# A fused transformer block on one core: other places for the products beside gating and quantising, and a part of each group's end moved into the next steps

## The chip, the cores and the metric

The kernel runs on one core of a Trainium2 chip. The metric is the device time of one execution in microseconds. Engines are named as the profile names them: TensorE (PE, with PEld for its weight loads), VectorE (DVE), ScalarE (ACT), GpSimd (POOL) and SyncE (SP), whose queue issues all transfers.

## The reference, cut to what matters

The input x is 2 x 2048 rows of 512. Four residual stages follow each other; each begins with a layer norm.

```python
x = x + tanh(g0) * softmax((n(x) @ W.T + b) @ (ctx @ W.T + b).T) @ ctx              # stage 1, ctx 77 x 512
x = x + tanh(g1) * ternary(gelu(ternary(n(x), w_up)), w_down)                       # stage 2, 512 -> 2048 -> 512
x = x + tanh(g2) * (attention(n(x), ctx, 16 heads of 32, 77 keys) @ Wout + bout)    # stage 3
x = x + tanh(g3) * fp4(silu(fp4(n(x), gate_w)) * fp4(n(x), up_w), down_w)           # stage 4, 512 -> 2048 -> 512
```

`ternary` divides its input by the root of the row's mean square and multiplies by weights of -1, 0 and 1. `fp4` quantises its input and its weights in blocks of 16: a scale in an 8-bit format from the block's largest magnitude, then eight magnitudes for each number.

## The kernel before

The 4096 rows are 8 groups of 512 rows; a group is 4 tiles of 128 rows. Every engine runs its own list of instructions in order, written out by hand, and waits on semaphores (`want(engine, name, group, count)`). Each engine walks the same loop of two phases.

`phase_a(g3, g1)` has 26 steps. It does stage 3 of group g3 (`attend`, one step for four heads of a tile, 16 in all, each passing through scores, row maximum, Exp, transposes and values in later steps; then on3, ott, oth/otl, out3 and x3 for each tile) and stage 1 of group g1 = g3 + 1 (`stage1`; a tile starts at the steps of `START1`). After stage 1 it takes the statistics and norm of stage 2, transposes the four tiles (`T2_AT`), and computes the first up products (`UP_AT`). In its last steps it also quantises the first half of stage 4's input of g3 (`X4_STEPS`).

`phase_b(g, s4)` has 33 slots. It does stage 2 of group g (16 up products of eight matmuls with 512 columns each, 16 down products of the same size, norm 3 and the query products) and stage 4 of group s4 = g - 1. Stage 4 has 16 units. A unit is a gate product and an up product of four matmuls each (`gate_up`), a tanh on ScalarE (`tanh4`) and two multiplications on VectorE (`hidden`); the next gate product waits for the first of them, since it writes the same bank. After four units the tile's 2048 hidden numbers are quantised on VectorE (`quant4`, parts 0 to 4: block maxima, scales, scaling, codes, last multiplication), transposed by a DMA (`turn_h`), multiplied by w_down (`down4`, 16 matmuls) and added (`out4`). `TILE_AT` says at which slot a tile's units start, `QUANT_AT` and `POST_AT` where quantising and the product stand. In a slot TensorE first issues a whole up product, then a whole down product (four chunks of a tile), then the gate pair.

For stage 2, ScalarE makes two gelus and a square of every up product, and GpSimd subtracts the rounded gelu from the exact one (L430); SyncE transposes both parts (`turn_ht`, L311). GpSimd also makes the roots of the norms (`root`, L406; `root4`, L411; L417, L436). The order of SyncE's queue is `turns`: input codes' transposes (L332), those of the gelus, of the hidden codes (L339), a store of half a group (L349), and the load of the next group but one (`load_x`, L252), which waits for stage 2's results.

In group 0's phase B there is no stage 4. In its place VectorE makes the codes of the stage 4 weights in 36 parts (`prepare`), spread over the slots (`PREP_AT`), and SyncE transposes them (L302, L298).

The lines of the profile that matter: L1109 is the helper `product` (up, gate, w_down, query and others; told apart by the operand names), L1196 the down product, L877 and L881 the two multiplications of `hidden`, L512 tanh, L500 and L503 the gelus, L545 Exp, L835 to L859 quantising, L696 statistics, L709 variance, L727 norm, L733 the low half of transposed rows, L865 stage 4's norm, L901 `out4`, L930 row maximum.

## Time and profile before

| | |
|---|---|
| time, median of 3 runs | 1780.79 us (1778.44 to 1780.8) |
| the profiled execution's own time | 1780.83 us |
| its span | 1779.0 us |
| TensorE busy | 1356.1 us, 76% |
| VectorE busy | 1409.3 us, 79% |
| ScalarE busy | 692.7 us, 39% |
| GpSimd busy | 243.1 us, 14% |

The span runs from the first instruction to the last. TensorE's busy time overlaps from one matmul to the next, so its share overstates. Shares are means over all stages; a group takes about 191 us in the steady part (from 490 to 1636 us), the start takes 290 us and the end, without a next group, 143 us.

### The profile page before, as it was taken

The numbers are of one execution on the slowest core, as the hardware profiler recorded it, in microseconds if no ns is written. First come the engines' busy times: TensorE is split into PE (matmuls) and PEld (weight loads), VectorE is DVE, ScalarE is ACT, GpSimd is POOL, SyncE is SP. The second block draws the span as 40 slices with busy tenths as digits, with TensorE's granted clock in tenths as the row PEclk, the third lists the DMA queues.
The fourth block names the chain that finished last, engine by engine and source line by source line (L and its number), as shares of the span: only waits on it lengthen the run. The fifth ranks groups of instructions, "written<-read, shape, count | busy, mean of one in ns | idle before, by whom it ended". The sixth has DMA issues, their size and how long they took to land.

```text
span 1779.0 us, 22434 instructions
## 1 busy us (share of the span) xinstructions
PE 1356.1 (76%) x8120; PEld 695.2 (39%) x8120; DVE 1409.3 (79%) x2440; ACT 692.7 (39%) x2106; POOL 243.1 (14%) x197
## 2 busy tenths in 40 slices
PE   5043737889787988698878978798879887997775
PEld 4021314434363435343443435343534354343421
DVE  6988886877887787878887788779787888786786
ACT  2113205542374326442554236432734164414420
POOL 1102200031002200131003100320023001310000
PEclk9556867999899999999999989999999999999987
DMA  9165862043202410053104320342013300521002
GB/s 349 70 236 136 191 171 47 1 71 60 71 2 43 87 50 25 8 88 83 25 1 78 53 71 2 60 72 57 16 30 66 83 25 7 89 45 40 7 18 59
DMA packets 267428, 119.69 MB, mean 67 GB/s; under 512 B 244122, under 2 KB 244634, under 8 KB 265782
## 3 DMA queue, kind: packets, MB, share of 16 engines
q1 hardware_dynamic: 267318, 118.27, 28.5%
q8 instruction: 64, 1.05, 0.2%
q14 instruction: 46, 0.38, 0.1%
HBM read 49.04 MB, written 8.39 MB: 32 GB/s over the span
## 4 chain that ended last, share of the span: by engine, by line
DVE 45%; PE 33%; ACT 8%; issue 6%; DMA 4%; SPq 2%; POOL 0%; DVEq 0%; ACTq 0%
PE bank L1109 25%; PE bank L1196 6%; ACT region L545 4%; DVE amax L835 4%; DVE hid L840 3%; DVE pair L844 3%; DVE stats L696 2%; DMA hqt<-pair 2%; DVE region L935 2%; DVE th L877 2%; DVE pair L859 2%; DVE region L727 2%; DVE pair L852 2%; DVE sr L810 2%; SPq L302 1%
## 5 line engine op out<-in xcount | busy, mean ns | idle before, releaser
L1196 PE MATMUL bank<-w_dn,region 128*128 128x512 fp8e4 x1024 | 243.7, 386 | 41.6 <-DMA region<-region 41.6
L1109 PE MATMUL bank<-w_up,xt 128*128 128x512 fp8e4 x1024 | 247.6, 389 | 31.3 <-ACT region L503 16.6
L1109 PE MATMUL bank<-w_gate,xqt 128*128 128x512 bf16 x512 | 146.8, 414 | 99.4 <-DVE th L877 56.3
L430 POOL TENSOR_TENSOR region<-g,region 128x512 f16<-128x512 f32 x128 | 178.2, 1396 | 297.5 <-ACT region L503 289.8
L545 ACT ACTIVATE region<-bank,nm 128x77 f32<-128x77 f32 x512 | 161.0, 353 | 66.8 <-DVE nm L930 66.8
L512 ACT ACTIVATE th<-bank,each 128x512 f32<-128x512 f32 x112 | 77.0, 687 | 271.7 <-PE bank L1109 271.7
L877 DVE SCALAR_TENSOR_TENSOR th<-th,bank 128x512 f32<-128x512 f32 x112 | 76.8, 686 | 129.5 <-ACT th L512 129.5
L500 ACT ACTIVATE g<-bank 128x512 f32<-128x512 f32 x128 | 76.4, 597 | 246.9 <-PE bank L1109 188.4
L1196 PEld LDWEIGHTS bank<-w_dn,region 128*128 128x128 f16 x1024 | 101.5, 99 | 167.5 <-DMA region<-region 43.1
L1109 PE MATMUL bank<-w_down,hqt 128*128 128x512 bf16 x496 | 132.2, 427 | 43.8 <-DMA hqt<-pair 43.8
L1109 PEld LDWEIGHTS bank<-w_up,xt 128*128 128x128 f16 x1024 | 101.6, 100 | 162.2 <-ACT region L503 20.5
L1109 PE MATMUL bank<-w_gup,xqt 128*128 128x512 bf16 x512 | 145.6, 411 | 8.8 <-DVE xin L888 4.6
L1146 PE MATMUL bank<-ident,region 128*128 128x128 f32 x384 | 60.1, 296 | 102.5 <-DVE region L727 84.7
L477 ACT ACTIVATE xt<-bank 128x512 f16<-128x512 f32 x96 | 55.4, 600 | 179.8 <-PE bank L1146 179.7
L545 ACT ACTIVATION_READ_ACCUMULATOR region<-bank,nm 128x1 f32 x512 | 119.6, 235 | 0.0
L1109 PEld LDWEIGHTS bank<-w_gate,xqt 128*128 128x128 bf16 x512 | 49.2, 103 | 175.9 <-DVE th L877 71.6
L1109 PEld LDWEIGHTS bank<-w_down,hqt 128*128 128x128 bf16 x496 | 52.6, 108 | 119.9 <-issue 75.1
L930 DVE TENSOR_REDUCE nm<-bank 128x4 f32<-128x308 f32 x128 | 59.8, 472 | 49.4 <-PE bank L1109 49.3
L1109 PE MATMUL bank<-w_o,region 128*128 128x512 f16 x384 | 92.2, 392 | 8.6 <-DVE region L945 8.6
L536 ACT ACTIVATE region<-bank 77x512 f16<-77x512 f32 x128 | 79.0, 617 | 37.3 <-PE bank L1267 37.3
L1146 PEld LDWEIGHTS bank<-ident,region 128*128 128x128 f32 x384 | 48.0, 152 | 114.6 <-issue 75.3
L1109 PE MATMUL bank<-xt,w_q 128*128 128x512 f16 x384 | 88.1, 388 | 1.4 <-DVE xt L733 1.4
(208 smaller groups left out, 2468.5 us busy)
## 6 DMA issues: line engine op xcount, KB each, us to landing
xin<-in_x SPq DMA_DIRECT2D x16, 512.0 KB, 4.6
out_x<-x SPq DMA_DIRECT2D x16, 512.0 KB, 2.9
region<-in_w_up_t SPq DMA_DIRECT2D x1, 4096.0 KB, 13.7
hid<-in_gate_w SPq DMA_DIRECT2D x4, 1024.0 KB, 5.3
x<-in_gate_w SPq DMA_DIRECT2D x4, 1024.0 KB, 6.1
...
```

The lines of the kernel that those rows point to most:

```text
L430: eng.tensor_tensor(hn[1][:, t % 2, ns], g32[:, s % 2, :], hn[0][:, t % 2, ns], ALU.subtract).then_inc(sg["hl"], 1)
L477: eng.activation(xt[0][:, :, t * P:(t + 1) * P], bank[t % 2][:, :].rearrange("p (k t) -> p k t", k=KD), ACT.Copy).then_inc(sg[f"xh{stage}" ...
L500: eng.activation(g32[:, s % 2, :], bank[s % 2][:, :], ACT.Gelu).then_inc(sg["g32"], 1)
L512: eng.activation(th[:, u % 2, :], bank[4][:, :], ACT.Tanh, scale=half_cg[:, :]).then_inc(sg["th"], 1)
L536: eng.activation(pt3[0][0:M, m % 2], bank[6 + m % 2][0:M, :].rearrange("p (h t) -> p h t", h=HC), ACT.Copy).then_inc(sg["p3h"], 1)
L545: last = eng.activation(p3[:, n % 2, j, :], bank[4 + n % 2][:, j * M:(j + 1) * M], ACT.Exp, bias=nm3[:, n % 2, j:j + 1], accum_out=rs3[:, ...
L835: done(eng.tensor_reduce(peaks, blocks, AX.X, ALU.max, apply_absolute_value=True))
L877: eng.scalar_tensor_tensor(th[:, u % 2, :], th[:, u % 2, :], 1.0, bank[4][:, :], ALU.add, ALU.mult).then_inc(sg["hg"], 1)
L930: eng.tensor_reduce(nm3[:, n % 2, :], bank[4 + n % 2][:, 0:HC * M].rearrange("p (h m) -> p h m", h=HC), AX.X, ALU.max, negate=True).then_i ...
L1109: last = mm(out, lhs, rhs, start=(n == 0), stop=(n == len(pairs) - 1))
L1146: last = tr(bank[t % 2][:, k * P:(k + 1) * P], xn[:, t, k * P:(k + 1) * P], ident[:, :])
L1196: last = mm(bank[2 + t % 2][:, :], ht[i][:, t % 2, f, :], w_dn[:, f, :], start=(f == 0 and i == 0), stop=(f == KF - 1 and i == 1))
```

## The change

Sizes and number of products, transposes and transfers stay the same. Only their places in the lists of the engines change, with a few instructions split.

- Phase A: stage 1 starts one step earlier (`START1`). Statistics and norm of stage 1 are halved: tiles 0 and 1 stay in the phase B before, tiles 2 and 3 go to steps 2, 3 and 5. All four tiles of stage 2 are transposed in one step, tiles 2 and 3 through banks 4 and 5 (`state_bank`). Eight up products follow instead of three, in the steps 18 to 25, and ScalarE's gelus of them stand in the same steps. The input quantising of stage 4 starts at step 19 instead of 21.
- The scores, row maxima and the first Exp of attention steps 0 and 1 are issued before phase A, around the last query product.
- The last multiplication of the last tile's codes is at step 2 of phase A, its w_down product at steps 4 to 7 in four quarters into bank 3 (`late_down`), its output at step 8. The other parts of that tile's quantising lie between the query steps of phase B.
- Phase B has 25 slots. Units and quantising alternate: slots 1 to 4, 6 to 9, 11 to 14 and 16 to 19 are units, 5, 10 and 15 quantise a whole tile. `FILL_AT` says which up and down products, whole or in halves of four matmuls, TensorE issues in each slot; they come behind the gate pair of the slot.
- GpSimd makes the second root of norm 4 after the seventh subtraction of stage 2 and no longer ahead of the first. SyncE turns the second half of the input codes after the first two tiles of stage 2. Store, transpose and load keep their order.

The diff, cut to its core (in the slot lists of VectorE and TensorE only the new lines are shown):

```diff
-START1 = (1, 2, 7, 8)
+START1 = (0, 1, 6, 7)
+STATS1_AT = {2: (2,), 3: (3,)}
+NORM1_AT = 5
+LATE_QUANT, LATE_DOWN, LATE_OUT = 2, (4, 5, 6, 7), 8
 VAR2_AT = START1[-1] + 7
 NORM2_AT = VAR2_AT + 2
-T2_AT = {NORM2_AT + 1: (0, 1), NORM2_AT + 2: (2, 3)}
-UP_AT = {NORM2_AT + 3: 0, NORM2_AT + 4: 1, NORM2_AT + 5: 2}
-VAR4_AT = TILES * NC + 3
+T2_AT = NORM2_AT + 1
+UPS_A = 8
+UP_AT = {T2_AT + 1 + i: i for i in range(UPS_A)}
+VAR4_AT = TILES * NC + 1
 X4_STEPS = {VAR4_AT + 2: (0, 1), VAR4_AT + 3: (2,), VAR4_AT + 4: (3,), VAR4_AT + 5: (4,)}
-STEPS = max(TILES * NC + 10, NORM2_AT + 6)
+STEPS = max(TILES * NC + 10, T2_AT + 1 + UPS_A)
 CHUNKS = F // D
 UP_SLOTS = TILES * CHUNKS
-SLOT_DOWN = 2 * CHUNKS
-SLOT_MS = {UP_SLOTS // 2 + 2: 0, UP_SLOTS + 2: 1}
-SLOT_DOWN2 = [SLOT_DOWN + CHUNKS * (t + 1) for t in range(TILES)]
-SLOT_NORM3 = SLOT_DOWN2[-1] + 1
-SLOT_T3, SLOT_Q = SLOT_NORM3 + 1, SLOT_NORM3 + 2
-SLOT_NORM1 = SLOT_Q + 2
-X4_AT = {1: (0, 1), 2: (2, 3), 3: (4,)}
-TILE_AT = (2, 9, 16, 23)
+TILE_AT = (1, 6, 11, 16)
 GU_AT = {TILE_AT[t] + n: 4 * t + n for t in range(TILES) for n in range(4)}
-QUANT_AT = {TILE_AT[t] + 4 + i: (t, q) for t in range(TILES) for i, q in enumerate(((0, 1, 2), (3, 4)))}
-POST_AT = {TILE_AT[t] + (10 if t < TILES - 1 else 7): t for t in range(TILES)}
-SLOTS = max([SLOT_Q + NC] + [s + 2 for s in POST_AT]) + 1
+QUANT_SLOTS = [TILE_AT[t] + 4 for t in range(TILES - 1)]
+UPS_AT = {0: (8,), 1: (9,), 2: (10,), 3: (11,), 5: (12, 13, 14), 7: (15,)}
+FILL_AT = {
+    0: (("up", 8, (0, 1)),), 1: (("up", 9, (0, 1)),), 2: (("up", 10, (0, 1)),), 3: (("up", 11, (0, 1)),),
+    5: (("down", 0, (0, 1)), ("up", 12, (0, 1)), ("down", 1, (0, 1)), ("up", 13, (0, 1)), ("down", 2, (0, 1)),
+        ("down", 3, (0, 1)), ("up", 14, (0, 1))),
+    6: (("up", 15, (0,)),), 7: (("up", 15, (1,)),), 8: (("down", 4, (0,)),), 9: (("down", 4, (1,)),),
+    10: tuple(("down", k, (0, 1)) for k in range(5, 10)), 11: (("down", 10, (0,)),), 12: (("down", 10, (1,)),),
+    15: tuple(("down", k, (0, 1)) for k in range(11, 16))}
+SLOT_MS, SLOT_RS = {5: 0, 10: 1}, {6: 0, 10: 1}
+SLOT_DOWN2 = [7, 11, 15, 16]
+SLOT_NORM3 = 17
+T3_AT = {17: (0, 1), 18: (2, 3)}
+SLOT_Q = TILE_AT[-1] + 4
+SLOT_STATS1, SLOT_NORM1 = SLOT_Q, SLOT_Q + 2
+X4_AT = {0: (0, 1), 1: (2,), 2: (3,), 3: (4,)}
+LAST_QUANT_AT = {SLOT_Q: 0, SLOT_Q + 1: 1, SLOT_Q + 3: 2, SLOT_Q + 4: 3}
+DOWN4_FIRST, DOWN4_LAST = {QUANT_SLOTS[1]: 0}, {QUANT_SLOTS[2]: 1, SLOT_Q: 2}
+OUT4_AT = {TILE_AT[3] + 2: 1, SLOT_Q + NC: 2}
+SLOTS = SLOT_Q + NC + 1
 TAIL_PARTS = ((0, 1), (2,), (3,), (4,))
-PREP_SLOTS = SLOT_NORM3 + 3
+PREP_SLOTS = SLOT_STATS1
 PREPS = [(m, q) for m in range(len(FP4_PIECES)) for q in range(2, QUANT_PARTS)]
 PREP_AT = {s: PREPS[len(PREPS) * s // PREP_SLOTS:len(PREPS) * (s + 1) // PREP_SLOTS] for s in range(PREP_SLOTS)}
-POOL_MS = {UP_SLOTS // 2 + 2: 0, UP_SLOTS: 1}
+POOL_MS = {UPS_A + 5: 0, UP_SLOTS: 1}
+ROOT4_AFTER = UPS_A - 2
...
             def turns(g, g1, g2):
-                for h in range(2):
-                    turn_x(g, h)
+                turn_x(g, 0)
                 if g1 is not None:
                     turn_ht(g1, 0)
                     turn_ht(g1, 1)
+                turn_x(g, 1)
...
+                    if s4 is not None and s == ROOT4_AFTER:
+                        root4(s4, 1)
...
+                    if g1 is not None and n in UP_AT:
+                        up(g1, UP_AT[n])
...
+                if n in STATS1_AT:
+                    for t in STATS1_AT[n]:
+                        tile_stats(1, g, xin, t)
+                    if STATS1_AT[n][-1] == TILES - 1:
+                        norm_stats(1, g, (2, 3))
+                if n == NORM1_AT:
+                    norm(1, g, xin, (2, 3))
...
+                    if g3 and n == LATE_QUANT:
+                        quant4(g3 - 1, TILES - 1, (4,))
+                    if g3 and n == LATE_OUT:
+                        out4(g3 - 1, TILES - 1, 3)
...
+                    if s in SLOT_DOWN2[:-1] and s4 is None:
+                        down2_stats(g, SLOT_DOWN2.index(s))
+                    if s == SLOT_DOWN2[-1]:
+                        down2_stats(g, TILES - 1)
+                        norm_stats(3, g)
                     if s == SLOT_NORM3:
                         norm(3, g, xb)
+                    if s4 is not None and s in X4_AT:
+                        if 0 in X4_AT[s]:
+                            x4(s4, 1)
+                        elif s in GU_AT:
+                            hidden(s4, GU_AT[s])
+                        quant_x4(s4, 1, X4_AT[s])
+                    for t in T3_AT.get(s - 1, ()):
+                        x_lo(3, g, t)
+                    if s4 is not None and s in GU_AT and s not in X4_AT:
+                        hidden(s4, GU_AT[s])
+                    if s == SLOT_STATS1 and g + 1 < GROUPS:
+                        stats1(g + 1)
                     if SLOT_Q < s <= SLOT_Q + NC:
                         c = s - SLOT_Q - 1
                         want(dve, "qh", g, c + 1)
                         eng.tensor_tensor(qt[1][:, c, :], q32[:, c % 2, :], qt[0][:, c, :],
                                           ALU.subtract).then_inc(sg["ql"], 1)
+                    if s == SLOT_NORM1 and g + 1 < GROUPS:
+                        norm(1, g + 1, xin, (0, 1))
+                    if s == SLOT_Q + NC - 1:
+                        row_max(g, 0)
+                        row_max(g, 1)
                     if s4 is None:
+                        if s in SLOT_MS:
+                            mean_square(g, SLOT_MS[s])
                         for m, q in PREP_AT.get(s, []):
                             prepare(m, q)
+                    if s4 is not None:
+                        if s in QUANT_SLOTS:
+                            t = QUANT_SLOTS.index(s)
+                            quant4(s4, t, (0, 1))
+                            if s in SLOT_MS:
+                                mean_square(g, SLOT_MS[s])
+                            quant4(s4, t, (2,))
+                        if s in SLOT_DOWN2[:-1]:
+                            down2_stats(g, SLOT_DOWN2.index(s))
+                        if s in LAST_QUANT_AT:
+                            quant4(s4, TILES - 1, (LAST_QUANT_AT[s],))
+                        if s in QUANT_SLOTS:
+                            if t == 1:
+                                out4(s4, 0)
+                            quant4(s4, t, (3, 4))
+                        if s in OUT4_AT:
+                            out4(s4, OUT4_AT[s])
+                    if s in SLOT_RS:
+                        root_scale(g, SLOT_RS[s])
...
+            def late_down(g, q):
+                if q == 0:
+                    want(pe, "qh", g + 1)
+                    want(pe, "hqt", g)
+                for k in range(4 * q, 4 * q + 4):
+                    last = mm(bank[3][:, :], hqt[:, k, :], w_down[:, k, :], start=(k == 0), stop=(k == KF - 1))
+                if q == 3:
+                    last.then_inc(sg["dn4"], 1)
...
+                    if s4 is not None and s in GU_AT:
+                        gate_up(s4, GU_AT[s])
+                    if s4 is not None and s in DOWN4_FIRST:
+                        down4(s4, DOWN4_FIRST[s])
+                    for kind, k, halves in FILL_AT.get(s, ()):
+                        if kind == "up":
+                            up(g, k, halves)
+                        else:
+                            down(g, *divmod(k, 4), s4 is None, halves)
+                    for t in T3_AT.get(s, ()):
+                        x_t(3, g, t)
+                    if s == SLOT_Q + NC - 1:
+                        scores(g, 0)
+                        scores(g, 1)
                     if SLOT_Q <= s < SLOT_Q + NC:
                         if s == SLOT_Q:
                             want(pe, "xl3", g)
                         query(g, s - SLOT_Q)
+                    if s4 is not None and s in DOWN4_LAST:
+                        down4(s4, DOWN4_LAST[s])
```

## Rows read from the trace of the kernel before

**Rows 1.** Busy time by stretch of one steady group (us, instructions, granted clock, DMA):

```profile
871.00:907.00 36.00, 31.04 (x370) 23.53 (x369) 28.53 (x63) 30.98 (x155) 0.00 (x0) 1.00 0.05 16
907.00:921.00 14.00, 9.71 (x98) 6.24 (x97) 12.72 (x34) 4.80 (x14) 2.33 (x2) 1.00 0.01 1
921.00:947.00 26.00, 16.99 (x69) 7.03 (x70) 21.41 (x44) 9.91 (x20) 5.84 (x5) 0.87 0.06 10
947.00:1012.00 65.00, 63.35 (x295) 28.61 (x293) 45.75 (x67) 26.95 (x58) 18.63 (x14) 1.00 0.48 86
1012.00:1062.00 50.00, 40.03 (x176) 17.71 (x175) 44.27 (x75) 11.37 (x17) 2.01 (x2) 0.90 0.21 53
sum 191.00, PE 161.12 PEld 83.12 DVE 152.68 ACT 84.03 POOL 28.81; mean PE 32.22 PEld 16.62 DVE 30.54 ACT 16.81 POOL 5.76
```

**Rows 2.** Waits from 871 to 1062: total us, times, longest:

```profile
DVE th L877 <- ACT th L512: 18.3, 11, 3.3
```

**Rows 3.** Chain (first, last), instructions and one microsecond's stretch at the group's end:

```profile
871.42 2.56 ACT region L545 x16
...
1051.00 1.72 SPq L339 DMA_TRANSPOSE hqt<-pair  x1
...
1054.00:1055.00 1.00, 0.00 (x0) 0.00 (x0) 0.97 (x6) 0.89 (x1) 0.00 (x0) 0.50 0.77 143
...
1055.41 5.96 PE L1109 MATMUL bank<-w_down,hqt 128*128 128x512 bf16 x16 [4.25 <-DMA hqt<-pair]
...
1062.57 2.56 ACT region L545 x16
```

**Rows 4.** Instructions in order of time, gating units: start, duration, engine, [idle before]:

```profile
1002.61 0.69 ACT L512 ACTIVATE th<-bank,each 128x512 f32<-128x512 f32 x1 [2.77 <-PE bank L1109]
1003.27 1.89 PE L1196 MATMUL bank<-w_dn,region 128*128 128x512 fp8e4 x8
1006.06 0.69 ACT L512 ACTIVATE th<-bank,each 128x512 f32<-128x512 f32 x1 [2.77 <-PE bank L1109]
...
1029.62 1.04 PE L1109 MATMUL bank<-w_gate,xqt 128*128 128x512 bf16 x4
1030.69 0.69 ACT L512 ACTIVATE th<-bank,each 128x512 f32<-128x512 f32 x1 [1.85 <-PE bank L1109]
```

**Rows 5.** Instructions in order of time: quantising one tile, first and last:

```profile
1011.90 3.62 PE L1109 MATMUL bank<-w_down,hqt 128*128 128x512 bf16 x16
...
1013.02 2.27 DVE L835 TENSOR_REDUCE amax<-hid 128x128 f32<-128x2048 f32 x1
...
1023.68 1.23 DVE L859 TENSOR_TENSOR pair<-pair,sc_b 128x2048 bf16<-128x2048 f16 x1
```

**Rows 6.** Instructions in order of time: the attention's end:

```profile
905.67 2.76 PE L1109 MATMUL bank<-w_o,region 128*128 128x512 f16 x12
...
920.83 0.99 DVE L865 TENSOR_SCALAR xb<-x,mv,rstd 128x512 f32<-128x512 f32 x2
...
933.79 0.69 POOL L411 TENSOR_TENSOR rstd<-ve,powers 128x2 f32<-128x2 f32 x1 [17.48 <-DVE ve L709]
934.45 3.75 POOL L430 TENSOR_TENSOR region<-g,region 128x512 f16<-128x512 f32 x3
934.52 2.67 DVE L865 TENSOR_SCALAR xb<-x,mv,rstd 128x512 f32<-128x512 f32 x2 [0.81 <-POOL rstd L411]
```

**Rows 7.** Instructions in order of time, and the load's view: SyncE's queue behind out4:

```profile
1024.83 0.74 DVE L901 SCALAR_TENSOR_TENSOR x<-bank,each,x 128x512 f32<-128x512 f32 x1
1026.08 3.37 SPq L339 DMA_TRANSPOSE hqt<-pair  x1
1029.49 1.11 SPq L252 DMA_DIRECT2D xin<-in_x  x2
DMA to landing us min/median/max: 3.7/4.1/4.4
```

**Rows 8.** Instructions in order of time: group 0's phase B:

```profile
183.97 4.55 SPq L311 DMA_TRANSPOSE region<-region  x2
185.97 1.22 DVE L859 TENSOR_TENSOR pair<-pair,w_down 128x2048 bf16<-128x2048 f16 x1 [5.73 <-DMA w_gate<-pair]
```

More of the change, by code:

```diff
@@ L527, in query, with powers_of @@
                                bias=bq[:, c:c + 1]).then_inc(sg["qh"], 1)
+            def powers_of(g, n):
+                want(act, "nm3", g, n + 1)
+                if n >= 2:
+                    want(act, "p3t", g, n - 1)
+                t, c = divmod(n, NC)
+                for j in range(HC):
+                    h = HC * c + j
+                    last = eng.activation(p3[:, n % 2, j, :], bank[4 + n % 2][:, j * M:(j + 1) * M], ACT.Exp,
+                                          bias=nm3[:, n % 2, j:j + 1], accum_out=rs3[:, t % 2, h:h + 1])
+                last.then_inc(sg["p3"], 1)
             def attend(g, n):
@@ L709, in norm_stats, with norm @@
                 eng.tensor_scalar(dst, mv[:, s, ts, 1], LN_EPS, None, ALU.add).then_inc(sg[f"var{stage}"], 1)
-            def norm(stage, g, src):
-                want(dve, f"rstd{stage}", g)
+            def norm(stage, g, src, tiles=range(TILES)):
+                want(dve, f"rstd{stage}", g, 1 + tiles[0] // 2 if stage == 1 else None)
                 scale = rstd[:, 0, :]
@@ L725, in norm @@
                     scale = rn[:, :]
-                for t in range(TILES):
+                for t in tiles:
                     eng.tensor_scalar(xn[:, t, :], src[:, t, :], mv[:, 0, t, 0:1], scale[:, t:t + 1],
@@ L1193, in down @@
                         want(pe, *(("on3", g - 1) if t == 0 else ("x3", g - 1)))
-                for f in range(4 * q, 4 * q + 4):
+                for f in [4 * q + 2 * h + j for h in halves for j in range(2)]:
                     for i in range(2):
@@ L1265, in attend @@
                         want(pe, "p3l", g, m - 1)
+                    elif m == 1 and g:
+                        want(pe, "out4", g - 1, TILES - 1)
                     for j in range(HC):
@@ L1315, in _ @@
             pe.wait_ge(sm["wt_done"], WT_DONE)
-            for g in range(GROUPS - 2):
+            for g in range(GROUPS - 1):
                 phase_a(g, g + 1)
```

229 lines of the change are left out of this document (104 added, 125 removed).

## The prediction

> **What bounds the kernel now.** I read the page first (its busy shares, TensorE 76% and VectorE 79%, say only that both matter), then a table of stretches of one steady group [rows 1], the waits inside it [rows 2], and the chain and the instructions in order of time. The chain returns to the first Exp of an attention every 191.15 us, 871.42 to 1062.57 [rows 3], and so it does for groups 2 to 7. In 191 us VectorE works 152.7 and is idle 38.3; TensorE, busy 161 by a measure that overlaps, is idle more often than it looks; ScalarE works 84 [rows 1]. So no engine is full, and VectorE is nearest. I count the group as VectorE's work plus VectorE's idle time. By stretch that idle time is 7.5 us in the attention (871 to 907), 1.3 and 4.6 in its end (to 921, to 947), 19.2 in gating and quantising (947 to 1012) and 5.7 after it [rows 1]. The largest named wait is for the tanh, 18.3 us in 11 waits [rows 2].
>
> Two patterns make it. In gating, tanh follows tanh at 3.45 us (1002.61, 1006.06), because TensorE puts a whole up or down product (1.73 us from start to start, 1.89 as printed) between two gate/up pairs; the loop alone is shorter: gate product from 1029.62, tanh from 1030.69 for 0.69, then VectorE's own 0.69, 2.5 us in all [rows 4]. Second, at the group's end the last hidden codes are made, transposed and multiplied in series before the scores: codes' transpose issued 1051.00, product 1055.41 for 5.96, first Exp 1062.57 [rows 3]. The granted clock there has fallen to 1.2 GHz after TensorE's idle 4.25 us; the product takes 5.96 us where the earlier one took 3.62 [rows 3, 5].
>
> **The change, part by part.** (1) *Gating units at their own pace.* Products are cut in halves (0.87 us), at most one half between pairs; whole products go into the quantising slots, where VectorE has 11.9 us of its own (1013.02 to 1024.91) [rows 5] and TensorE gets seven products or five and a down product: 7 x 1.73 = 12.1, and 5 x 1.73 + 3.46 = 12.1. The two are balanced. A pair of 2 x 0.87 plus a half is 2.6 us. New VectorE waits: tile 0 (slots 1 to 3 still carry whole products, but VectorE has the second half of the input's codes there) 2.0; tiles 1 and 2: a first unit free, then three at 2.6 plus 1.4 is 9.2, less work 7.4 and 6.9, so 1.8 and 2.3; tile 3 none, since norm 3, its splits and down2 lie between the units. Sum 6.0 for 18.3. Bounds: 3 (each unit at once) to 18 (spacing stays 3.45).
>
> (2) *Eight up products in the attention's end instead of three.* This uses TensorE where it idles. But GpSimd's second root for norm 4 used to stand before its subtractions (933.79, then 934.45) [rows 6] and now stands after the seventh. From the first up product, TensorE has the third and fourth output products (2.8 plus 0.4 of values each [rows 6]), the transposes of the fourth (0.5) and seven ups (12.1) before that; then two gelus 1.1, one subtraction 1.4, the root 0.7: 22.2 us. VectorE, from the same point, has three splits, half the input's codes, on3, x3 and statistics, a wait of 2.4 for the last output product, and arrives after about 17.4. So it waits 4.8 for the root, with x4 and all quantising behind it. Idle here 2.4 + 4.8 = 7.2; bounds 0.8 (the root's wait before, and nothing else) and 12. The first gate product no longer waits for the input's transpose.
>
> (3) *First norm halved and moved; loads.* VectorE reads xin two slots after the load can be issued. SyncE's order is kept: store after the second out4, transpose, then the load. Before: out4 starts 1024.83 and ends at 1025.57, transpose 1026.08 taking 3.37 of the queue, loads 1029.49 to 1030.6, landing 3.7 after the issue: about 1034.3, 8.7 us after out4 [rows 7]. Then nobody needed it until 1052. Now VectorE has after that out4 two splits (1.3) and one unit (1.4) and then stands at the statistics: wait 8.7 - 2.7 = 6.0 us, with the amax of tile 3, the query's splits and both row maxima behind it. Bounds 0 and 9. It happens in six groups (the last loads nothing).
>
> (4) *Last codes, product and output inside the attention.* Off the path go the 4.25 us transpose wait, the 5.96 product and one out4. VectorE, however, was nearly full there (idle 5.7 in 50 us), so what it regains is those 5.7 less new gaps: the last query product behind the second scores 0.5, and 1.0 for a slow clock in front of unit 13, where TensorE now idles some 4 us (its 12.1 us of fill end before VectorE's quantising and down2, 13.3, and the next down2 and norm 3 statistics). The moved work (half a norm, one multiplication, one out4: 4.5 us) goes where VectorE was 28.5 of 36 busy [rows 1]; minus two row maxima that left. Attention idle: 3.5 by walking the steps with no latency but ScalarE's late start, 7.5 if all of it stays. I take 5.5. The late product's 3.5 us of TensorE in four quarters hide there.
>
> (5) *Added work.* One more variance instruction and its waits: 0.5 us. Port: next to a GpSimd subtraction the same x4 instruction pair takes 2.67 us where without it 1.0 [rows 6]; more subtractions now lie beside the input's quantising. I add 3.0 (three such delays at about 1 each; bounds 0 and 8). The Trainium skill (SBUF — State Buffer, section SBUF: two separate sides) says the pair of ports shared by VectorE and GpSimd is an exclusive lock for a whole instruction, so that the loser blocks fully. By that rule each of the eight subtractions in the attention's end can hold one instruction for its full length, and the term would be up to 11; the 2.67 agrees with the rule in kind, and the length depends on how they fall.
>
> Sum for a steady group: work 152.7 + 0.5 + 3.0 = 156.2; idle 6.0 + 7.2 + 6.0 + 5.5 + 0.5 + 1.0 and 2.8 of small gaps (38.3 less the waits that the view names) = 29.0; together 185.2, a gain of 5.9.
>
> (6) *The ends.* Last group (7): no load, no next norm; the serial product goes as a whole. From tile 2's codes to the second Exp 37.8 us before, 28.5 now, so 9; and 7 from the gating: gain 16. Tail: input codes finish one to two steps ahead of the last x3, 4 less; the late product's work 2 more: gain 2. Group 0: root_scale(0) now stands after the twelfth of the 36 preparing parts, and waits for the thirteenth up's subtraction, which waits for the transpose of tile 1 (issued 183.97 for 4.55, landed about 191), then 0.6 + 1.4 + 0.7. That is 194, where VectorE is free at 187.2 [rows 8]; with the down product behind it, loss 8; bounds 0 and 15.
>
> Groups 1 to 6: 6 x 5.9 = 35; 35 + 16 + 2 - 8 = 45. The profiled execution took 1780.83 for its span of 1779.0, the median of the runs shown is 1780.79, so no shift: 1780.8 - 45 = 1736.
>
> **Rivals.**
> *Gating doesn't tighten* (slower). For: no two tanhs of the trace come nearer than 3.4 us while products are interleaved; ScalarE now has gelus between them and each half product needs the ones before it. If the units stay at 3.45, ten of them cost 0.85 each, 8.5 x 7 groups = 60: 1796. It decides at a spacing of about 3.25; from there the stalls of (2) and (3) eat the rest. Against: the 2.5 us loop of [rows 4].
> *Port contention doubled.* The three delays are eight: 5 more per group, 7 groups, 35: 1771. For: [rows 6]. Against: subtractions are as many as before, and the total of VectorE's work before contains some five such delays.
> *The stalls don't come.* xin lands, and the root is ready, before VectorE gets there, since its work ahead runs later than I walk it. Half of 6.0 and 4.8 saved: 5.4 x 6.5 groups = 35: 1701. Against: both places follow from issue order, and VectorE's lateness would itself cost.
> *It cancels.* The moved work takes the attention's slack wholly (7.5) and the small gaps grow with more handshakes by 4: 6 a group, about 1778.
>
> **Chances.** Forecast 0.52, port 0.12, no stalls 0.13, cancelling 0.06, gating 0.17. About 0.2% (3.6 us) is what a measurement can tell from no change. Of cancelling 0.05 lies within it and 0.01 is faster. So faster 0.78, same 0.05, slower 0.17. The forecast's own range is 1718 to 1756; the range to 8 in 10 reaches the port rival wholly, to 1704 for half the no-stall case, and to 1786 for cancelling: 1704 to 1786.
>
> **What would show it.** Period from Exp to Exp: 185, not 191. Tanh spacing 2.6 in tiles 1 and 2. VectorE waiting for DMA xin about 6 us before the statistics, six times; for GpSimd's rstd about 5 us before x4. The wait of TensorE for hqt at the end gone. In group 0 a VectorE wait for rms of some 7 us. Wrong if tanh spacing stays over 3.2, if the xin wait is under 2 or over 9, or if VectorE's work in a group rises by over 8 us.

## The result

The changed kernel takes 1756.37 us in the median of four runs (1747.85 to 1767.32), the kernel before 1780.6: ratio 0.9874, 95% interval 0.9831 to 0.9918. It is faster, by 24 us where 45 were forecast (1736); the time lies within the range. The four runs lie 1.1% apart, those of before 0.13%. The profiled execution is the slowest of the four, 1767.32, with a span of 1765.5, so the two profiles differ by 13.5 us where the medians differ by 24.

### The profile page after: what moved, and what is told of

Same layout as the page of the kernel before. It is cut to its first block, busy times and chain, and to the rows that moved or that the text cites. A ratio compares the mean times of both kernels' runs of the same rounds, so it can differ in the third digit from the quotient of the medians.

```text
span 1765.5 us, 22470 instructions
## 1 busy us (share of the span) xinstructions
PE 1356.3 (77%) x8053; PEld 702.2 (40%) x8120; DVE 1413.7 (80%) x2448; ACT 692.1 (39%) x2106; POOL 261.6 (15%) x205
## 4 chain that ended last, share of the span: by engine, by line
DVE 37%; PE 29%; issue 5%; ACT 5%; DMA 3%; SPq 1%; POOL 1%; DVEq 0%; POOLq 0%; ACTq 0%
PE bank L1171 18%; PE bank L1271 4%; DVE amax L876 4%; PE bank L1256 3%; DVE stats L723 3%; DVE pair L885 2%; DVE th L918 2%; DVE hid L881 2%; DVE region L979 2%; DVE xt L760 2%; DVE pair L895 2%; DVE sr L851 2%; DMA xin<-in_x 2%; DVE pair L893 2%; DMA hqt<-pair 1%
## 5 line engine op out<-in xcount | busy, mean ns | idle before, releaser
L1271 PE MATMUL bank<-w_dn,region 128*128 128x512 fp8e4 x1024 | 235.7, 383 | 30.3 <-DMA region<-region 30.3
L452 POOL TENSOR_TENSOR region<-g,region 128x512 f16<-128x512 f32 x128 | 164.5, 1289 | 321.5 <-ACT region L526 314.2
L1171 PE MATMUL bank<-w_gate,xqt 128*128 128x512 bf16 x475 | 139.3, 414 | 76.1 <-DVE th L918 74.2
L1271 PEld LDWEIGHTS bank<-w_dn,region 128*128 128x128 f16 x1024 | 100.8, 99 | 154.2 <-DMA region<-region 31.2
L918 DVE SCALAR_TENSOR_TENSOR th<-th,bank 128x512 f32<-128x512 f32 x112 | 76.7, 684 | 74.7 <-ACT th L535 74.7
L1171 PE MATMUL bank<-w_down,hqt 128*128 128x512 bf16 x370 | 92.6, 404 | 27.1 <-DMA hqt<-pair 26.4
L559 ACT ACTIVATION_READ_ACCUMULATOR region<-bank,nm 128x1 f32 x512 | 111.9, 219 | 0.0
L1171 PE MATMUL bank<-xt,w_q 128*128 128x512 f16 x384 | 93.2, 399 | 7.4 <-DVE xt L760 7.4
L1171 PE MATMUL bank<-keys,region 128*128 128x308 f16 x384 | 75.2, 307 | 18.8 <-DVE region L1044 15.9
L1211 PEld LDWEIGHTS bank<-ident,region 128*128 128x128 f32 x384 | 51.7, 161 | 94.5 <-issue 61.2
L1358 PE MATMUL bank<-ident,region 128*77 128x128 f32 x512 | 85.5, 292 | 2.1 <-DVE x L942 2.1
```

The source lines that it names most:

```text
L452: eng.tensor_tensor(hn[1][:, t % 2, ns], g32[:, s % 2, :], hn[0][:, t % 2, ns], ALU.subtract).then_inc(sg["hl"], 1)
L559: last = eng.activation(p3[:, n % 2, j, :], bank[4 + n % 2][:, j * M:(j + 1) * M], ACT.Exp, bias=nm3[:, n % 2, j:j + 1], accum_out=rs3[:, ...
L918: eng.scalar_tensor_tensor(th[:, u % 2, :], th[:, u % 2, :], 1.0, bank[4][:, :], ALU.add, ALU.mult).then_inc(sg["hg"], 1)
L1171: last = mm(out, lhs, rhs, start=(n == 0), stop=(n == len(pairs) - 1))
L1211: last = tr(state_bank(stage, t)[:, k * P:(k + 1) * P], xn[:, t, k * P:(k + 1) * P], ident[:, :])
L1271: last = mm(bank[2 + t % 2][:, :], ht[i][:, t % 2, f, :], w_dn[:, f, :], start=(f == 0 and i == 0), stop=(f == KF - 1 and i == 1))
```

## The profile after

First the page's shares: span, then busy us, share and instructions of each engine.

```profile
span 1765.5 us, 22470 instructions
PE 1356.3 (77%) x8053; PEld 702.2 (40%) x8120; DVE 1413.7 (80%) x2448; ACT 692.1 (39%) x2106; POOL 261.6 (15%) x205
```

VectorE's work has not shrunk (1413.7 us for 1409.3 before), so the gain of the profiled pair (13.5 us) is idle time of VectorE, 351.8 us for 369.7. Next the steady group that answers to [rows 1] and [rows 2]. It runs from 959.8 to 1148.4, between the same two instructions of neighbouring groups. The view of busy time by stretch has, for each engine, busy us and instructions, then granted clock, DMA share and GB/s; the five parts are the end of the units of tile 3, a wait, quantising beside the query, the attention and its end.

```profile
1021.80:1036.40 14.60, 11.24 (x45) 6.00 (x47) 12.32 (x25) 4.34 (x7) 1.01 (x1) 0.77 0.11 35
1036.40:1043.20 6.80, 4.67 (x17) 1.67 (x16) 0.00 (x0) 1.27 (x2) 0.00 (x0) 0.81 0.99 236
1043.20:1060.60 17.40, 12.94 (x68) 6.73 (x66) 16.80 (x29) 9.08 (x26) 0.70 (x1) 0.97 0.00 0
1060.60:1097.30 36.70, 32.96 (x362) 23.86 (x365) 30.87 (x74) 26.65 (x133) 0.70 (x1) 0.95 0.12 30
1097.30:1130.50 33.20, 28.62 (x189) 15.14 (x187) 25.81 (x52) 20.26 (x49) 11.66 (x11) 1.00 0.22 41
...
959.80:1148.40 188.60, 162.21 (x993) 84.63 (x1001) 153.78 (x280) 84.00 (x262) 31.01 (x24) 0.95 0.23 48
```

The group takes 188.6 us: VectorE works 153.8 (152.7 before) and is idle 34.8 (38.3). Its waits in that window, from the view of waits (total us, times, longest):

```profile
DVE th L918 <- ACT th L535: 9.7, 10, 1.6
DVE stats L723 <- DMA xin<-in_x: 6.8, 1, 6.8
DVE xb L906 <- POOL rstd L434: 4.5, 1, 4.5
DVE xin L793 <- PE bank L1171: 3.0, 2, 2.8
DVE x L996 <- PE bank L1171: 2.1, 2, 1.9
DVE nm L960 <- PE bank L1171: 2.0, 3, 1.2
```

The tanh wait of [rows 2], 18.3, has become 9.7, and two waits that were under 1 us have come, for the load and for GpSimd's root. Here is the first in order of time (start, duration, engine and line, idle before it and its releaser). SyncE's queue stands as in [rows 7]: store behind out4, a transpose, then the load.

```profile
1033.12 0.74 DVE L942 SCALAR_TENSOR_TENSOR x<-bank,each,x 128x512 f32<-128x512 f32 x1
...
1033.89 0.38 SPq L368 DMA_DIRECT2D out_x<-x  x1
1034.38 3.35 SPq L358 DMA_TRANSPOSE hqt<-pair  x1
1037.77 1.11 SPq L271 DMA_DIRECT2D xin<-in_x  x2
...
1043.23 1.29 DVE L723 BATCH_NORM_STATS2 stats<-xin 128x6 f32<-128x512 f32 x2 [6.85 <-DMA xin<-in_x]
```

And the second, that answers to [rows 6]: the variance is there at 1126, and GpSimd takes two subtractions, which wait for gelus, ahead of the root.

```profile
1125.89 0.17 DVE L736 TENSOR_SCALAR ve<-mv 128x2 f32<-128x2 f32 x1
...
1126.98 1.16 POOL L452 TENSOR_TENSOR region<-g,region 128x512 f16<-128x512 f32 x1 [5.34 <-ACT region L526]
1128.71 1.16 POOL L452 TENSOR_TENSOR region<-g,region 128x512 f16<-128x512 f32 x1 [0.57 <-ACT region L526]
1129.82 0.70 POOL L434 TENSOR_TENSOR rstd<-ve,powers 128x2 f32<-128x2 f32 x1
...
1130.55 1.83 DVE L906 TENSOR_SCALAR xb<-x,mv,rstd 128x512 f32<-128x512 f32 x2 [4.49 <-POOL rstd L434]
```

A third thing was not in the forecast. These are the gate products of unit 1 of two groups, from the list of TensorE in order of time. In both TensorE had waited 3.09 us for VectorE; once the product takes 1.89 us, once 1.04.

```profile
946.10 1.89 PE L1171 MATMUL bank<-w_gate,xqt 128*128 128x512 bf16 x4 [3.09 <-DVE th L918]
947.78 1.91 PE L1171 MATMUL bank<-w_gup,xqt 128*128 128x512 bf16 x4
...
1137.51 1.04 PE L1171 MATMUL bank<-w_gate,xqt 128*128 128x512 bf16 x4 [3.09 <-DVE th L918]
1138.38 1.03 PE L1171 MATMUL bank<-w_gup,xqt 128*128 128x512 bf16 x4
```

The granted clock of these two places, from the view of stretches, is 0.50 (1.2 GHz) and 1.00 (2.4 GHz):

```profile
1138.00:1140.00 2.00, 2.00 (x11) 0.93 (x10) 1.99 (x3) 0.69 (x1) 0.00 (x0) 1.00 0.00 0
946.00:948.00 2.00, 1.91 (x5) 0.74 (x6) 1.86 (x3) 0.00 (x0) 0.00 (x0) 0.50 0.00 0
```

Where the clock fell, the stretch from the fourth tile's codes to the next tile 0's is 103.7 us (869.56 to 973.28), in the other group 100.8 (1061.00 to 1161.83). All six such stretches of this trace follow the clock of that pair: 103.7 twice where both products ran at half, 102.8 once where only the second did, 100.8 to 101.0 three times where neither did. So groups of 188.5 and of 191 us stand side by side. Before the change that stretch is 110.0 us in five of six groups (112.2 in the first). So the changed kernel has a source of spread that the old one lacks.

## The experiments

All ran beside the kernel before (1778 to 1781 us); the changed kernel itself was not run beside them again. Changes of time are differences of medians to its 1756.4, whose own interval is some 8 us to either side; the kernels that build on one another are compared with each other. Where places in a profile are compared, it is one execution of each kernel. Units are counted from 0 to 15, so unit 5 is the second of tile 1 and unit 13 the second of tile 3.

**1. The load in front of the store** (1717.87 us; ratio 0.966, 0.9647 to 0.9673).

```diff
                 turn_h(g, 1)
-                store(g, 0)
                 turn_h(g, 2)
                 if g2 is not None:
                     want(sp, "x2", g1)
                     load_x(g2)
+                store(g, 0)
```

> SyncE's list is reordered: the third tile's code transpose and the next xin load now stand in front of the first store (before: store, transpose, load). The load can then start when the last x2 is made (1022.5 in the steady group) and not after out4(1) at 1033.9. Theory A, VectorE's waits add up: the six xin waits of 6.8 us go and nothing takes their place: 41 us less, about 1715. Theory B, TensorE's queue decides there: down4(2) starts only some 2.2 us earlier (its own wait for hqt, 2.13) and runs at full clock (1.7 less), the query products and the first scores behind it move by those 4 us, and VectorE waits for the rest at the splits of the query and at the row maxima: 4 x 6 = 24 us less, about 1732, with the sum of its waits at these lines up by 2 to 3 us a group. Theory C, the time comes back elsewhere: within 5 us of 1756.

38.5 us less: theory A, nearly in full. SyncE's list and VectorE's, for the same load as above:

```profile
993.70 1.98 SPq L358 DMA_TRANSPOSE hqt<-pair  x1
995.74 1.47 SPq L271 DMA_DIRECT2D xin<-in_x  x2
1003.37 0.38 SPq L368 DMA_DIRECT2D out_x<-x  x1
...
1005.17 0.69 DVE L922 TENSOR_TENSOR hid<-th,bank 128x512 f32<-128x512 f32 x1
1005.78 1.28 DVE L723 BATCH_NORM_STATS2 stats<-xin 128x6 f32<-128x512 f32 x2
```

The load is issued 7.6 us before the store and not 3.9 behind it; the statistics follow the last unit at once. Of 48.5 us of such waits only group 0's 7.7 is left. The splits of the query (L1044) wait 20.8 us in the whole run instead of 16.0. That TensorE's queue would take over (theory B) was wrong: at that place its wait for the transpose, 2.13 us before, went with the same edit, and the w_down product behind it takes 3.62 us for 5.30.

**2. The root after the fifth subtraction** (1725.11 us; 0.9695, 0.9678 to 0.9713).

```diff
-ROOT4_AFTER = UPS_A - 2
+ROOT4_AFTER = UPS_A - 4
```

> GpSimd's second root of norm 4 stands after the fifth subtraction instead of the seventh. The statistics are ready at 1125.9, the fifth subtraction ended at 1121.6, so rstd would be there at 1126.7 and not at 1130.5. Theory A: VectorE's wait falls from 4.5 to about 1.0 and all behind it moves up: 3.3 x 7 groups = 23 us less, about 1733. Theory B: the input's amax, scaling and codes now run beside the sixth to tenth subtractions and are slowed one by one (1.0 each), so only half comes: about 1745. Theory C: TensorE's first gate products are the bound there and the wait moves to th: within 5 us of 1756.

31.3 us less, more than theory A's 23. The place itself gives what was expected (in order of time, the same group as above):

```profile
1095.11 0.17 DVE L736 TENSOR_SCALAR ve<-mv 128x2 f32<-128x2 f32 x1
1095.35 0.70 POOL L434 TENSOR_TENSOR rstd<-ve,powers 128x2 f32<-128x2 f32 x1 [4.27 <-DVE ve L736]
1096.09 1.84 DVE L906 TENSOR_SCALAR xb<-x,mv,rstd 128x512 f32<-128x512 f32 x2 [0.81 <-POOL rstd L434]
```

Whole run, the root's wait goes from 32.3 to 6.5 us, and the tanh wait from 74.7 to 58.6, which the edit doesn't touch. VectorE's work grew by 7 us, theory B's contention, but far below half the gain. What comes on top of 23 us stands in the list of TensorE, at the gate product of unit 1:

```profile
1104.19 1.04 PE L1171 MATMUL bank<-w_gate,xqt 128*128 128x512 bf16 x4 [0.56 <-DVE th L918]
```

With the root earlier, TensorE idles at most 0.56 us ahead of unit 1 and not 3.09, and the pair runs at full clock in all seven groups. The six stretches that were 100.8 to 103.7 us are now 97.9 to 99.9, 22 us less together. Unit 5's pair, too, ran at full clock in four groups, and there tile 0's codes to tile 1's take 22.2 us and not 23.7 to 23.9: 7 us less together.

**3. Both edits** (1688.0 us; 0.9489, 0.9476 to 0.9502).

> Both edits together (load in front of the store, root after the fifth subtraction). The two places are 70 us apart in a group. If the effects are independent, the gain is the sum of the two single ones: 41 + 23 = 64 (1692) where all waits add up, 24 + 23 = 47 (1709) where TensorE's queue limits the first. If a common bound outside stands behind them (TensorE's total work, the clock), it is clearly less than the sum.

68.4 us less; the single gains add up to 69.8. So two idle places of VectorE 70 us apart are independent, within the changed kernel's spread; no bound outside them shows.

**4. The last product put back** (1822.64 us; 1.0256, 1.0237 to 1.0275).

```diff
-DOWN4_FIRST, DOWN4_LAST = {QUANT_SLOTS[1]: 0}, {QUANT_SLOTS[2]: 1, SLOT_Q: 2}
+DOWN4_FIRST, DOWN4_LAST = {QUANT_SLOTS[1]: 0}, {QUANT_SLOTS[2]: 1, SLOT_Q: 2, SLOT_Q + NC: 3}
...
+                            if s == SLOT_Q + NC:
+                                quant4(s4, TILES - 1, (4,))
                             out4(s4, OUT4_AT[s])
+                            if s == SLOT_Q + NC:
+                                out4(s4, TILES - 1)
...
-                    if g3 and n == LATE_QUANT:
-                        quant4(g3 - 1, TILES - 1, (4,))
-                    if g3 and n == LATE_OUT:
-                        out4(g3 - 1, TILES - 1, 3)
...
-                    if g3 and n in LATE_DOWN:
-                        late_down(g3 - 1, LATE_DOWN.index(n))
```

> The late part is undone alone: last multiplication of the fourth tile's codes, its transpose, the whole down product and its out4 stand before the third scores again (as before the change); everything else of the change stays. Theory of the prediction: a transpose wait of 4.3, a product of 3.6 to 6 us and an out4 of 0.7 return to the path, less the idle time that VectorE has at that place (0.4 row maximum, PE wait 4) and in the attention: 6 to 9 us a group, 7 groups, 42 to 63: 1798 to 1819, so the late part alone is more than the whole measured gain and the rest of the change cost. Rival: VectorE is the line and its work is the same either way, the attention takes the product's 4 quarters in return for as much delay (it waits 4.1 for xt there and 2.8 for out3): 2 to 3 us a group, about 1772.

66 us more, 9.5 a group, a little above the 6 to 9 of the prediction's theory and far from the rival's 2 to 3. TensorE and VectorE at that place, and VectorE's waits of this kind in the whole run:

```profile
1090.15 4.56 PE L1171 MATMUL bank<-w_down,hqt 128*128 128x512 bf16 x15 [10.79 <-DMA hqt<-pair]
...
1094.75 0.75 DVE L942 SCALAR_TENSOR_TENSOR x<-bank,each,x 128x512 f32<-128x512 f32 x1 [8.74 <-PE bank L1171]
...
DVE x L942 <- PE bank L1171: 64.7, 7, 10.3
```

So the late part alone is worth more than the whole change brought. Without it the change would be 45 us slower than the kernel before (1778.0 beside it).

**5. Whole products between the pairs again** (1768.65 us; 0.9942, 0.9927 to 0.9957).

```diff
-UPS_AT = {0: (8,), 1: (9,), 2: (10,), 3: (11,), 5: (12, 13, 14), 7: (15,)}
+UPS_AT = {0: (8,), 1: (9,), 2: (10,), 3: (11,), 5: (12, 13), 7: (14,), 8: (15,)}
...
-        ("down", 3, (0, 1)), ("up", 14, (0, 1))),
-    6: (("up", 15, (0,)),), 7: (("up", 15, (1,)),), 8: (("down", 4, (0,)),), 9: (("down", 4, (1,)),),
-    10: tuple(("down", k, (0, 1)) for k in range(5, 10)), 11: (("down", 10, (0,)),), 12: (("down", 10, (1,)),),
+        ("down", 3, (0, 1)),),
+    6: (("up", 14, (0, 1)),), 7: (("up", 15, (0, 1)),), 8: (("down", 4, (0, 1)),), 9: (("down", 5, (0, 1)),),
+    10: tuple(("down", k, (0, 1)) for k in range(6, 8)), 11: (("down", 8, (0, 1)),), 12: (("down", 9, (0, 1)),),
+    13: (("down", 10, (0, 1)),),
```

> The gating spacing undone alone: in tiles 1 and 2 a whole product (1.73 us) stands between gate/up pairs again where the change put a half or nothing (seven halves more between units per group), and the quantising slots carry five and two products fewer halves. Theory A, the filler sets the unit's pace: spacing back from 2.53 to 3.45, 0.92 for each of six spacings, 5.5 a group, 7 groups: 39 us slower, about 1795, and VectorE's th wait up from 74.7 to about 112. Theory B, only the first unit after quantising (its gate product at half clock behind 2.7 us of idle) limits these tiles, the others have slack: at most 10 us slower, about 1766.

12.3 us more, just over theory B's bound of 10 and far from theory A's 39; VectorE's tanh waits are 88.2 us in the whole run, not 112 (74.7 in the changed kernel). Tile 1's tanhs as VectorE takes them, first here, then in the changed kernel:

```profile
1170.74 0.69 DVE L919 SCALAR_TENSOR_TENSOR th<-th,bank 128x512 f32<-128x512 f32 x1 [1.51 <-ACT th L536]
1174.91 0.69 DVE L919 SCALAR_TENSOR_TENSOR th<-th,bank 128x512 f32<-128x512 f32 x1 [1.16 <-ACT th L536]
1178.36 0.69 DVE L919 SCALAR_TENSOR_TENSOR th<-th,bank 128x512 f32<-128x512 f32 x1 [2.04 <-ACT th L536]
```

```profile
1166.43 0.69 DVE L918 SCALAR_TENSOR_TENSOR th<-th,bank 128x512 f32<-128x512 f32 x1 [1.51 <-ACT th L535]
1170.41 0.69 DVE L918 SCALAR_TENSOR_TENSOR th<-th,bank 128x512 f32<-128x512 f32 x1 [1.02 <-ACT th L535]
1172.95 0.69 DVE L918 SCALAR_TENSOR_TENSOR th<-th,bank 128x512 f32<-128x512 f32 x1 [1.13 <-ACT th L535]
```

The last spacing is 3.45 and not 2.54, as theory A says. The middle one is 4.17 for 3.98, because down2 and its statistics lie there, and the first unit waits the same 1.51. So the filler sets the pace of about one unit in three here.

**6. Three halves in front of unit 5** (1738.98 us; 0.978, 0.9767 to 0.9792).

```diff
-    6: (("up", 15, (0,)),), 7: (("up", 15, (1,)),), 8: (("down", 4, (0,)),), 9: (("down", 4, (1,)),),
-    10: tuple(("down", k, (0, 1)) for k in range(5, 10)), 11: (("down", 10, (0,)),), 12: (("down", 10, (1,)),),
+    6: (("up", 15, (0, 1)), ("down", 4, (0,))), 8: (("down", 4, (1,)),),
+    10: tuple(("down", k, (0, 1)) for k in range(5, 10)), 11: (("down", 10, (0, 1)),),
```

> The same halves, but three of them stand in front of the gate product of unit 5 (one was there) and both halves of down 10 in front of unit 9's, none in the slots behind: TensorE's idle of 2.72 us ahead of unit 5 shrinks to about 1.0. Theory A: the granted clock then stays at full, unit 5's gate and up products take 1.03 each and not 1.89 and 1.81, VectorE's wait of 1.51 there goes, and units 6 and 7 lose a little of theirs: 1.5 to 2 us in each group that has the half clock there: 8 to 12 less, about 1746, and the runs lie closer together than the 1.1% of this kernel. Theory B: the clock falls elsewhere in return, or the th waits move on to the next unit: within 4 us of 1756.

17.4 us less, more than theory A asked, and the runs lie 0.4% apart. The gate product of unit 5 in the changed kernel, and here:

```profile
1163.71 1.89 PE L1171 MATMUL bank<-w_gate,xqt 128*128 128x512 bf16 x4 [2.72 <-DVE th L918]
```

```profile
1145.15 1.04 PE L1171 MATMUL bank<-w_gate,xqt 128*128 128x512 bf16 x4 [1.00 <-DVE th L918]
```

In all seven groups TensorE idles 1.0 us there and the pair runs at full clock. From tile 0's to tile 1's codes it is 21.7 us in every group (23.9 in the changed kernel), from tile 1's to tile 2's 23.2 (23.4); together some 17 us in seven groups. By the 22.2 us of experiment 2, where the idle time had stayed at 2.72 and the clock had not fallen, the clock is about 1.6 of the 2.2 us a group.

**7. Group 0's root one subtraction earlier**, on top of experiment 3 (1691.99 us; 0.9509, 0.9494 to 0.9524).

```diff
-                    if s + 1 in POOL_MS:
-                        a = POOL_MS[s + 1]
+                    if s4 is None and s + 1 == UPS_A + 4 or s + 1 in POOL_MS and (s4 is not None or s + 1 == UP_SLOTS):
+                        a = POOL_MS.get(s + 1, 0)
```

> On top of the two edits of the run with load and root (1688.0): in group 0 alone GpSimd takes the root for rms(0) after the twelfth subtraction instead of the thirteenth, which waits for a transpose. It is then there at 187.1, not 192.2. Theory A (the prediction's): VectorE's wait of 6.9 is the loss of group 0, so 5 us come back: 1683. Theory B: the down product that the next instruction reads ends at 194.4 in any case, so the wait moves from rms to dn and 0 to 1 us comes back: 1687 to 1688, with a wait of some 5 us at L825.

No gain against 1688.0 (the runs overlap: 1687.57 to 1695.57 and 1685.39 to 1688.87). That is theory B, with 6.6 us at L825 for its 5; the wait has only changed its name:

```profile
187.59 0.17 DVE L816 TENSOR_SCALAR rr<-rms 128x2 f32<-128x2 f32 x1 [1.74 <-POOL rms L460]
...
194.82 0.75 DVE L825 SCALAR_TENSOR_TENSOR xb<-bank,rr,xin 128x512 f32<-128x512 f32 x1 [6.60 <-PE bank L1271]
```

**8. Load, root and the fill of experiment 6** (1682.62 us; 0.9458, 0.9446 to 0.9471).

> Load in front of the store, root after the fifth subtraction, and three halves in front of unit 5 as in the run with the fill alone. If each effect is independent, this is 1688 less what the fill gives there (8 to 12): about 1678. If TensorE's half clock ahead of unit 5 had already gone in some groups with the two edits (its tile 0 to tile 1 spacing is 22.2 in some groups and 23.7 in others), the gain is 1.5 us times the groups that still have it, 2 to 4 of them: 1682 to 1685.

5.4 us less than experiment 3, as the second case says: four groups of that kernel still had a spacing of 23.5 to 23.9 us, three had 22.2; all have 21.7 now.

**9. Tile 0's products in halves too.** On the changed kernel with the fill of experiment 6: 1724.19 us (0.9693, 0.9675 to 0.971). On top of experiment 8: 1675.78 us (0.9417, 0.94 to 0.9435).

```diff
-UPS_AT = {0: (8,), 1: (9,), 2: (10,), 3: (11,), 5: (12, 13, 14), 7: (15,)}
+UPS_AT = {0: (8,), 1: (9,), 2: (10,), 4: (11,), 5: (12, 13, 14), 7: (15,)}
...
-    0: (("up", 8, (0, 1)),), 1: (("up", 9, (0, 1)),), 2: (("up", 10, (0, 1)),), 3: (("up", 11, (0, 1)),),
+    0: (("up", 8, (0, 1)),), 1: (("up", 9, (0, 1)), ("up", 10, (0,))), 2: (("up", 10, (1,)),),
+    3: (("up", 11, (0,)),), 4: (("up", 11, (1,)),),
```

> On the changed kernel, without the load and root edits: three halves in front of unit 5 (that alone gave 1739.0) and in tile 0 three halves in front of unit 1 instead of two, one half each between units 1, 2 and 3, the last half behind unit 3. TensorE's idle of 3.09 us ahead of unit 1's gate product becomes about 2.2. Theory A, that idle is what lets the clock fall in some groups and not in others (unit 1's pair takes 1.89 and 1.91 in one group, 1.04 and 1.03 in another, behind the same idle): the stretch from the fourth tile's codes to the next tile 0's codes, 100.8 to 103.8 us in these runs, is short in every group (10 us less in all) and the two waits behind units 1 and 2 fall by 1.5 a group (10 us): about 1718. Theory B, the clock in the attention's end has another cause: only the 10 us of waits: about 1729, with 101 to 104 as before.

> The same tile 0 edit on top of load, root and fill (1682.6), where that stretch is 98.3 us in nearly every group. Theory A: VectorE waits 1.23 and 1.44 for the tanh of units 2 and 3 because a whole up product stands between the pairs; a half instead takes 1.5 off each group: 1672. Theory B: TensorE has no idle time to give there, what goes between units is late in the quantising slot: within 3 us of 1682.

The first takes 14.8 us off experiment 6, between its two theories. The stretch from the fourth tile's codes is now 97.9 us in five of six groups and 99.6 in one, where it was 101 to 103.8. TensorE idles 2.2 us ahead of unit 1. The pair runs at full clock in six of seven groups; in the group of the 99.6 us it still fell:

```profile
1106.93 1.77 PE L1172 MATMUL bank<-w_gate,xqt 128*128 128x512 bf16 x4 [2.23 <-DVE th L919]
```

So the uneven clock at unit 1 is rarer in this trace, and not gone. Tile 0 to tile 1 is back at 23.6 from 21.7, which theory A had not counted. The second takes 6.8 us off, for the same reason less than its 10: 98.3 became 95.5 to 96.9, 21.7 became 23.6.

**10. Down 10 in the third quantising slot**, on top of experiment 9's second kernel (1669.38 us; 0.9381, 0.9368 to 0.9394), **and then one half less in front of unit 5** (1667.76 us; 0.9356, 0.9338 to 0.9373).

```diff
-    10: tuple(("down", k, (0, 1)) for k in range(5, 10)), 11: (("down", 10, (0, 1)),),
-    15: tuple(("down", k, (0, 1)) for k in range(11, 16))}
+    10: tuple(("down", k, (0, 1)) for k in range(5, 10)), 15: tuple(("down", k, (0, 1)) for k in range(10, 16))}
```

> As the run before, and the down product 10 moves from in front of unit 9 to the third quantising slot, behind which TensorE idles 3.54 us ahead of unit 13 and then runs its pair at half clock (1.89, 1.91). Theory A: idle 1.8, pair at full clock, VectorE's waits of 0.15, 0.37 and 0.69 in tile 3 go, and unit 9 comes a little sooner: 1.5 us a group, 10 less than the run before. Theory B: the next thing in tile 3 (ScalarE's copy of the transposes, 0.72) holds it: at most 4 less.

```diff
-    6: (("up", 15, (0, 1)), ("down", 4, (0,))), 8: (("down", 4, (1,)),),
+    6: (("up", 15, (0, 1)),), 8: (("down", 4, (0,)),), 9: (("down", 4, (1,)),),
```

> On top of the last run (load, root, fills, down 10 later; 1669.4): one half product less in front of unit 5. There the tile 0 edit had turned the balance: unit 5's gate product starts right behind the fill (921.19, no idle before it) and VectorE waits 1.71 us for its tanh; the spacing from tile 0's to tile 1's codes is 23.6 us where it was 21.7. Theory A, the half (0.87) delays the unit and can be taken behind unit 7: 0.9 to 1.9 a group, 6 to 13 less: 1656 to 1663. Theory B: the half is then late in front of unit 9 and comes back there: within 3 us of 1669.

The first gives 6.4 us, between its theories. Unit 13's gate product, in the changed kernel and here:

```profile
1024.49 1.89 PE L1171 MATMUL bank<-w_gate,xqt 128*128 128x512 bf16 x4 [3.54 <-DVE th L918]
```

```profile
968.02 1.04 PE L1171 MATMUL bank<-w_gate,xqt 128*128 128x512 bf16 x4 [1.81 <-DVE th L918]
```

The second gives nothing that can be told from no change: its time is theory B's. In the profiles 23.6 became 22.7, as theory A says, and 23.2 became 23.4; from group 1's first codes to the last group's last it is 5.1 us shorter. But the start up to those first codes is 4.7 us longer in this one execution (394.14 for 389.46), and of its lists the edit moves one half product. Whether a gain of 5 us hides in that spread is open. These two are the fastest kernels, 6% under the kernel before and 5% under the changed one.

## Why the prediction was right, and where its sizes were off

The mechanism was right: VectorE's idle time is the line, the stalls of steps 2 and 3 stand where they were put, and the sign follows. The size was off by half: 24 us, not 45. Between the two profiled executions the six groups from group 1's to group 7's codes of tile 2 gave 12.5 us where 35 were forecast: they take 188 to 191 us and not 185. What follows is one group of 188.6 us in the slowest of the four runs, 3.4 over the forecast's 185.2: idle 34.8 for 29.0, work 153.8 for 156.2.

1. *Gating.* 6.0 us was the sum of the waits, 9.7 + 0.7 is measured, the largest miss: tile 0 2.7 (2.0 forecast), tile 1 3.9 (1.8), tile 2 2.5 (2.3), tile 3 about 1.2 (none). The spacing is 2.53 in tile 2, as forecast. Tile 1's excess is in "a first unit free, then three at 2.6". The first unit was free, but of the three spacings behind it only the last was 2.54 (the rows of experiment 5: 3.98, then 2.54). The forecast had fill and quantising balanced; in fact TensorE was out of work for 2.72 us ahead of unit 5, and then ran its pair at 1.2 GHz. I had counted a slow clock for unit 13 alone, 1.0. Experiment 6 prices the idle time ahead of unit 5, clock and wait together, at 17 us; experiment 9 adds 15 for tile 0's fill, net of 1.9 us a group that it loses at tile 1. The rival of a gating that stays at 3.45 is out. Its price was too high as well: six spacings a group at 0.85 each would be 36 us by its reckoning, and whole products between those units cost 12.
2. *Root.* 4.5 + 2.1 measured, 4.8 + 2.4 forecast. Experiment 2 gives 31 us back where 3.3 x 7 = 23 was the wait's size. The rest goes with the idle time ahead of unit 1, which went from 3.09 to 0.56 us, and with the clock, which no longer fell there in any group; the forecast had neither.
3. *Load.* 6.8 measured, 6.0 forecast, in six groups; experiment 1 gives 38.5 of the 41.
4. *Late part.* The attention's idle time is 5.8 of 36.7 us (5.5 forecast), and experiment 4 prices the part at 66 us.
5. *Added work.* 1.1 us for 3.5: port contention was oversized, since the kernel before already had most of it. VectorE's instructions that are printed longer than others of their shape, nearly all beside a GpSimd instruction, add up to 5.3 us above the usual in the group before and 7.1 in this one. So the rival of doubled contention is out too. The small gaps were undersized, about 4.5 for 2.8. By the Trainium skill (SBUF — State Buffer, section SBUF: two separate sides), whose exclusive lock would have given up to 11, the term was larger still. The section limits the lock to VectorE's instructions in a 2-port mode or with two SBUF inputs, and lets whichever engine starts first go on; the 11 took each of the eight subtractions as a block of VectorE, so it was an upper bound. The trace agrees with the narrower reading: beside a subtraction a reduction keeps its 1.22 us (L876), and the x4 pair takes 1.83 for 0.99 (L906).
6. *The ends.* From the last group's tile 2 codes on 3.6 us were gained where 11 were forecast (9 and the tail's 2). The forecast took the late product as hidden there too. But the last group has no next group's work beside its attention, and the product's first quarter waits for its transpose with the scores behind it. The list of TensorE, and VectorE's row maximum:

```profile
1630.42 1.48 PE L1301 MATMUL bank<-w_down,hqt 128*128 128x512 bf16 x3 [2.04 <-DMA hqt<-pair]
...
1632.97 0.48 DVE L960 TENSOR_REDUCE nm<-bank 128x4 f32<-128x308 f32 x1 [4.75 <-PE bank L1171]
```

   Group 0's wait for rms is 7.36 (7 forecast), and its loss of 8 was written down to it; experiment 7 shows that the wait is not the cause, the down product is ready no sooner. The start up to group 1's codes of tile 2 became 2.7 us longer, where the forecast's 8 less 7 from the gating make 1. This is largely the one execution: up to group 1's first codes the kernel of experiment 1 has the same lists, and reached them at 395.63 us where this one took 403.22 (before 392.76). That alone would be 7.6 of the 11 us by which this execution lies above the median.

The rival "the stalls don't come" was wrong as a forecast but right in its price: it put half of both stalls at 35 us, and taking both away gives 68. The budget: 66 from the late part and about 28 from the rest of the moves, less 70 for the two stalls that the change made, is 24. The 28 is what is left over, not measured by itself.

## What to carry to other kernels

When an engine's idle time is the line, list what each moved step newly stands behind in every queue. Here an order left as it was (a store in front of a load) and a place chosen two subtractions too late (the root) took back three quarters of the gain, and moving one call and changing one constant returned it. A wait that is merely earlier than the next late thing gives nothing when it goes (experiment 7); walk to the next reader's other operand before pricing it. Fill TensorE's idle time in front of the product that others wait for, not behind it.

## What the chip showed beside this

The same idle time, 3.09 us ahead of unit 1's gate product, was followed by 1.2 GHz in one group and by 2.4 GHz in the next. In the seven groups of the changed kernel the pair of unit 1 ran wholly at half clock in three, wholly at full clock in three, and fell between its two products in one. Ahead of unit 13 TensorE idles 3.54 us; the pair ran at half clock in five groups and at full clock in two, as here:

```profile
1212.94 1.04 PE L1171 MATMUL bank<-w_gate,xqt 128*128 128x512 bf16 x4 [3.54 <-DVE th L918]
```

Behind 2.72 us (unit 5) the pair was slowed, in part or wholly, in all seven groups of the changed kernel, but ran at full clock in four of experiment 2. Behind 2.2 us (unit 1, experiment 9) it fell in one group of seven. Behind 1.8 us (unit 13, experiment 10) and 1.0 us (unit 5, experiment 6) it fell in none. So the idle time just ahead of a pair does not decide alone; what does is open. The changed kernel's runs lay 1.1% apart, those of the kernels made from it 0.2 to 0.6%; that the clock at units 1 and 5 makes the spread is likely, but was not shown run by run.
